# Bar rows built at a quarter of their width and earlier on GpSimd, with a thinner fill of the value tile

## The chip, the cores and the metric

One core of a Trainium2 chip runs the whole program. The metric is the device time of one execution in microseconds; the number compared is the median over several executions. A profile is one further execution, seen instruction by instruction.

## The reference

The input x is 8 sequences of 512 tokens with 128 channels. It is normalised, and two branches read the result:

```
xn = layernorm(x)                                # 8 x 512 x 128
s  = attention(xn): Q,K,V = relu(xn @ W + b); 16 heads of 8 channels,
     causal softmax, times V, plus xn, normalised again, gamma, beta
g  = silu(ffn(xn)): second norm, @ attn_w.T + b + residual,
     8 experts (128 -> 512 -> 128, gelu), @ next_w.T + b, gelu
out = x + s * g
```

The top-k of the router in the reference is computed and not used. Keys and queries whose row of xn sums to exactly zero are masked.

## The kernel before

The program has two stages with a barrier between them. In stage one (to about 183 us of the span) the statistics and normalised rows of x are made, then for each of the 8 sequences (i = 0 to 7) the projections Q, K and V, the split of Q and K into three bf16 parts that are stored to DRAM, and the whole feed-forward branch. In stage two the attention runs, 32 units of four heads. Each engine has its instruction order written out by hand, and semaphores join the engines. GpSimd and VectorE also wait on themselves after nearly every instruction (`link`).

**Causal mask.** Instead of a mask on the scores, 48 extra rows ("bar rows") are appended to the contraction of queries and keys. `bar_k` and `bar_q` hold them, 48 x 512 bf16 each. The pattern depends only on the token's place within its tile of 128, so the four tiles (TB = 4) are alike. `bar_rows` fills each with a constant and then overwrites it by `below`, an `affine_select`, three times for `bar_k` and four times for `bar_q`. Their only reader is `load_fixed` on SyncE, which waits for `bars_ready` when i is 1.

**GpSimd in stage one**, in order: constants, two identity matrices, a fill of `v_all` with 1.0 (L298) and then the release of `consts`, for which TensorE (two) and ScalarE (one) wait; seven linked operations on the bias rows (L312 to L318); `second_roots` for the first group of 8 tiles (twelve small operations that start once VectorE has sent `seeds_ready`); `bar_rows`; then `totals(i)`, six small operations that end in `sums_ready`. `v_all` is 128 x 32 x 144 in float32: for each head 8 value columns and one column of ones. ScalarE writes the value columns later (L574).

**VectorE in stage one**, in order: mean, variance and roots of the first 8 tiles, `quotients(0)`, `second_seeds`, `sums(0)`, `quotients(1)`, `sums(1)`, `rests` of sequence 0 (L484), means of the other 24 tiles (L91 to L401), `lows` of sequence 0 (L491, waits for ScalarE's L603), then variances and roots of the 24 tiles (from L408), and from there sequence by sequence.

**ScalarE and TensorE.** After the first projections ScalarE copies V out (L574) and waits for `sums_ready` before `second_norm(0)` (L536). TensorE then transposes that (L630), and multiplies (L649, L652); ScalarE adds the bias (L554), and the experts follow (L697, L707 on TensorE, L597 and L603 on ScalarE). At i = 1 TensorE runs 28 and 40 products without use (`hold`, L662), which keep it busy while it waits for VectorE.

Of the kernel before, what the change touches and what calls it, by code (L numbers as in the profile page):

```python
# [17 lines left out]
ALU = mybir.AluOpType  # L18
# [3 lines left out]
P = 128  # L22
B, T, C = 8, 512, 128
HEADS, DH = 16, 8
# [3 lines left out]
TB = T // P  # L28
# [8 lines left out]
VW = DH + 1  # L37
# [3 lines left out]
BLOCK = 3  # L41
BAR_ROWS = 48
# [3 lines left out]
BAR_KEYS = (0.0, 2.0 ** -37, 2.0 ** 13, 2.0 ** 63)  # L46
BAR_QUERIES = (-2.0 ** 62, -2.0 ** 12, -2.0 ** -38)
# [57 lines left out]
def build_program(nc, ctx, x, wq, wk, wv, wattn, wnext, w1, w2, cols, rows, out):  # L105
    def sb(name, shape, dt=F32, where=ctx):
        return where.enter_context(nc.sbuf_tensor(name, shape, dt))

    def sem(name):
        return ctx.enter_context(nc.semaphore(name))  # L110
# [12 lines left out]
    v_all = sb("v_all", [P, NT, HEADS * VW])  # L123
# [5 lines left out]
    bar_q = sb("bar_q", [BAR_ROWS, T], BF16)  # L129
    bar_k = sb("bar_k", [BAR_ROWS, T], BF16)  # L130
# [34 lines left out]
    def load_mask(sp, b, par, g, done):  # L165

        src = mask_dram[bass.ds(b * TB, TB), :].rearrange("n t -> (n t)")
        sp.dma_start(kx[par][MROW:MROW + 1, g],
                     src.unsqueeze(0).unsqueeze(0).broadcast_to([1, G, T])).then_inc(done, 16)
# [13 lines left out]
    with ExitStack() as one:  # L183
# [40 lines left out]
        blank, consts = sem("blank"), sem("consts")  # L224
# [20 lines left out]
        mean, var, a, y, t, s, sh, sl, r, nr, rem, v2, y2, t2 = (small[:, k, :] for k in range(14))  # L245

        with nc.Block() as block:
# [37 lines left out]
            @block.gpsimd  # L285
            def _(pool):
                pool.memset(ident[:, :], 0.0).then_inc(blank, 1)
                pool.memset(ident_b[:, :], 0.0).then_inc(blank, 1)
                pool.memset(ones_p[:, :], 1.0).then_inc(blank, 1)
                pool.memset(ones_b[:, :], 1.0).then_inc(blank, 1)  # L290
                pool.memset(bias_rows[:, :, :], 0.0).then_inc(blank, 1)
                pool.memset(q_fixed[:, :, :], 0.0).then_inc(blank, 1)
                pool.wait_ge(blank, 6)
                pool.memset(q_fixed[:, 0, :], 1.0).then_inc(blank, 1)
                for t in (ident, ident_b):
                    pool.affine_select(out=t[:, :], in_=t[:, :], compare_op=ALU.not_equal, fill=1.0, base=0,
                                       pattern=[[-1, P]], channel_multiplier=1).then_inc(blank, 1)
                pool.memset(v_all[:, :, :], 1.0).then_inc(blank, 1)  # L298
                pool.wait_ge(blank, 10)
                pool.sem_inc(consts, 2)  # L300

                chain = [0]

                def link(ins):
                    chain[0] += 1
                    ins.then_inc(pool_self, 1)
                    pool.wait_ge(pool_self, chain[0])


                pool.wait_ge(rows_in, 16)  # L310
                both = rows_sb[:, 0:2, :]
                link(pool.tensor_copy(bias_part[:, 0], both))  # L312
                link(pool.tensor_tensor(bias_rest[:, :, :], both, bias_part[:, 0], ALU.subtract))
                link(pool.tensor_copy(bias_part[:, 1], bias_rest[:, :, :]))
                link(pool.tensor_tensor(bias_part[:, 2], bias_rest[:, :, :], bias_part[:, 1], ALU.subtract))
                for p in range(PARTS):
                    on_p = slice(32 * p, 32 * p + 1)
                    link(pool.tensor_copy(bias_rows[on_p, :, :], bias_part[on_p, p]))  # L318
                pool.sem_inc(bias_ready, 1)

                def below(bar, k, value, sign=1):

                    link(pool.affine_select(out=bar[:, :].rearrange("p (n t) -> p n t", t=P),
                                            in_=bar[:, :].rearrange("p (n t) -> p n t", t=P),
                                            compare_op=ALU.is_ge, fill=value, base=-k * sign,
                                            pattern=[[0, TB], [sign, P]], channel_multiplier=-BLOCK * sign))

                def bar_rows():

                    link(pool.memset(bar_k[:, :], BAR_KEYS[BLOCK]))  # L330
                    for k in range(BLOCK, 0, -1):
                        below(bar_k, k, BAR_KEYS[k - 1])
                    link(pool.memset(bar_q[:, :], BAR_QUERIES[BLOCK - 1]))
                    for k in range(BLOCK - 1, -1, -1):
                        below(bar_q, k, BAR_QUERIES[k - 1] if k > 0 else 0.0)
                    below(bar_q, BLOCK - 1, 0.0, -1)
                    pool.sem_inc(bars_ready, 1)

                tt = pool.tensor_tensor

                def second_roots(tok, group):

                    at = slice(group[0], group[0] + group[1])
                    pool.wait_ge(seeds_ready, tok.next(seeds_ready))
                    for _ in range(3):
                        link(tt(t2[:, at], y2[:, at], y2[:, at], ALU.mult))
                        link(tt(t2[:, at], t2[:, at], v2[:, at], ALU.mult))
                        link(pool.tensor_scalar(t2[:, at], t2[:, at], -0.5, 1.5, ALU.mult, ALU.add))
                        link(tt(y2[:, at], y2[:, at], t2[:, at], ALU.mult))

                def totals(tok, i):

                    at = slice(TB * i, TB * i + TB)
                    pool.wait_ge(lanes_ready, tok.next(lanes_ready))
                    v = s16[:, at, :].rearrange("p n (a b l) -> p n a b l", a=2, b=2)
                    link(tt(s8[:, at, :, :], v[:, :, :, 0, :], v[:, :, :, 1, :], ALU.add))  # L356
                    link(tt(s4[:, at, :], s8[:, at, 0, :], s8[:, at, 1, :], ALU.add))
                    v = s4[:, at, :].rearrange("p n (a b) -> p n a b", b=2)
                    link(tt(s2[:, at, :], v[:, :, :, 0], v[:, :, :, 1], ALU.add))
                    link(tt(rem[:, at], s2[:, at, 0], s2[:, at, 1], ALU.add))  # L360
                    link(pool.tensor_scalar(shift[:, at], rem[:, at], -1.0 / C, None, ALU.mult))
                    link(tt(shift[:, at], shift[:, at], y2[:, at], ALU.mult))
                    pool.sem_inc(sums_ready, 1)

                tok = Tokens(pool)
                for i in range(B):
                    if i == 0:
                        second_roots(tok, GROUPS[0])
                        bar_rows()
                    if i == 2:  # L370
                        second_roots(tok, GROUPS[1])
                    totals(tok, i)
                pool.wait_ge(maskT_ready, 1)
                pool.dma_start(mask_dram, maskT[:, :]).then_inc(mask_out, 16)
                pool.wait_ge(mask_out, 16)
                for g in range(NG):
                    load_mask(pool, 0, 0, g, mask_in)
                pool.wait_ge(mask_in, 16 * NG)
                for g in range(NG):
                    pool.sem_inc(stack_in[0][g], 16)  # L380

                pool.sem_inc(blank, -10)
# [879 lines left out]
```

## Time and profile before

| | us |
|---|---|
| median of 3 executions | 456.26 (455.87 to 466.83) |
| the profiled execution's own time | 457.67 |
| its span, first to last instruction | 455.6 |
| TensorE busy | 383.3 (84%) |
| VectorE busy | 373.1 (82%) |
| ScalarE busy | 289.2 (63%) |
| GpSimd busy | 179.1 (39%) |
| mean granted TensorE clock | 0.970 |

The span starts at 0 with the first instruction; all times of rows count from there. Busy shares are averages over both stages. PE is TensorE, ACT ScalarE, DVE VectorE, POOL GpSimd.

### The profile page before, as it was taken

How to read it: one execution, taken by the hardware profiler on the slowest of the kernel's cores; microseconds unless marked ns; L12 is line 12 of the kernel's file. 1: busy time of each engine (PE TensorE's matmuls, PEld its weight loads, DVE VectorE, ACT ScalarE, POOL GpSimd, SP SyncE). 2: the span in 40 equal slices, each digit the busy share in tenths (PEclk: the TensorE clock that was granted, in tenths of full speed). 3: DMA queues.
4: the chain of work that ended last, by engine and by line, in shares of the span. 5: the costliest groups of instructions: out<-in, count | busy, mean ns of one | idle time of the engine just before them, and what ended most of it. 6: DMA issues, size and time to landing. Idle time of an engine off the chain costs nothing.

```text
span 455.6 us, 9692 instructions
## 1 busy us (share of the span) xinstructions
PE 383.3 (84%) x3541; PEld 249.3 (55%) x3541; DVE 373.1 (82%) x865; ACT 289.2 (63%) x580; POOL 179.1 (39%) x446
## 2 busy tenths in 40 slices
PE   0041899889999998899999999999999999999850
PEld 0021575457877775456656656665666566566420
DVE  5899388977778921899899999898999998989427
ACT  0122481278898884167777877877778778778740
POOL 9237000411111002311236547456556383565591
PEclk9997599999999999999999999999999999999995
DMA  8910030077644534723233342423332424340000
GB/s 238 316 52 1 0 100 0 0 170 160 156 112 115 139 98 116 128 57 86 81 90 79 82 109 73 118 63 105 92 96 64 129 56 113 79 110 27 4 24 23
DMA packets 31413, 41.72 MB, mean 92 GB/s; under 512 B 5910, under 2 KB 23686, under 8 KB 31366
## 3 DMA queue, kind: packets, MB, share of 16 engines
q1 hardware_dynamic: 31206, 41.08, 34.6%
q8 instruction: 28, 0.46, 0.4%
q14 instruction: 19, 0.16, 0.1%
q0 software_dynamic: 160, 0.03, 0.0%
HBM read 26.43 MB, written 11.02 MB: 82 GB/s over the span
## 4 chain that ended last, share of the span: by engine, by line
PE 43%; DVE 13%; issue 2%; ACT 1%; POOL 1%; DVEq 0%; ACTq 0%; POOLq 0%
PE banks L1152 15%; PE banks L1135 8%; DVE mx L951 8%; PE banks L1115 8%; PE banks L1117 5%; PE banks L1137 5%; DVE stats L996 2%; PE banks L1162 2%; DVE res L990 1%; ACT pt L1070 1%; PE banks L1124 0%; DVE res L977 0%; DVE res L980 0%; DVE mixed L981 0%; DVE aggr L1000 0%
## 5 line engine op out<-in xcount | busy, mean ns | idle before, releaser
L951 DVE TENSOR_REDUCE mx<-banks 128x1 f32<-128x512 f32 (+3 forms) x352 | 200.0, 633 | 19.9 <-PE banks L1117 18.2
L1070 ACT ACTIVATE pt<-banks 128x512 f32<-128x512 f32 x320 | 169.2, 601 | 44.2 <-PE banks L1137 36.7
L1152 PE MATMUL banks<-pt,vg 128*18 128x512 f32 (+3 forms) x1024 | 81.4, 436 | 0.7 <-ACT pt L1070 0.7
L1115 PE MATMUL banks<-k_own,q_own 76*128 76x384 bf16 (+2 forms) x192 | 48.4, 274 | 5.4 <-DVE mx L951 2.7
L1115 PE MATMUL banks<-w_room 76*128 76x384 bf16 (+2 forms) x192 | 48.1, 274 | 3.3 <-DVE mx L951 3.3
L842 POOL TENSOR_SCALAR mneg<-mx 128x16 f32<-128x16 f32 x32 | 8.1, 254 | 107.7 <-DVE mx L951 106.6
L1135 PE MATMUL banks<-w_room 76*128 76x384 bf16 (+2 forms) x192 | 47.5, 275 | 0.9 <-ACT pt L1070 0.5
L1135 PE MATMUL banks<-q_own,k_own 76*128 76x384 bf16 (+2 forms) x192 | 47.8, 274 | 0.0
L1152 PEld LDWEIGHTS banks<-pt,vg 128*18 128x18 f32 x1024 | 23.7, 97 | 43.8 <-issue 33.4
L1117 PE MATMUL banks<-k_own,q_own 124*128 124x128 bf16 x256 | 44.0, 219 | 0.0
L1117 PE MATMUL banks<-w_room 124*128 124x128 bf16 x256 | 43.8, 219 | 0.0
L1137 PE MATMUL banks<-q_own,k_own 124*128 124x128 bf16 x256 | 42.5, 219 | 0.0
L1137 PE MATMUL banks<-w_room 124*128 124x128 bf16 x256 | 42.2, 219 | 0.0
L697 PE MATMUL banks<-xaT,w_room 128*128 128x256 f32 x128 | 31.3, 401 | 0.8 <-ACT xaT L554 0.8
L707 PE MATMUL banks<-hid,w_room 128*128 128x256 f32 x128 | 29.2, 380 | 2.7 <-ACT hid L597 2.7
L624 PE MATMUL banks<-ident,xn_all 128*128 128x128 f32 x32 | 5.3, 292 | 27.9 <-DVEq L455 27.9
L697 PEld LDWEIGHTS banks<-xaT,w_room 128*128 128x128 f32 x128 | 25.2, 202 | 5.9 <-ACT xaT L554 2.4
L491 DVE TENSOR_TENSOR parts<-rest,parts 128x512 bf16<-128x512 f32 x16 | 11.1, 693 | 20.4 <-ACT parts L603 19.9
L707 PEld LDWEIGHTS banks<-hid,w_room 128*128 128x128 f32 x128 | 24.2, 190 | 6.4 <-ACT hid L597 3.2
L1115 PEld LDWEIGHTS banks<-k_own,q_own 76*128 76x128 bf16 x192 | 18.4, 97 | 16.5 <-DVE mx L951 8.9
L597 ACT ACTIVATE hid<-banks,cols_sb 128x256 f32<-128x256 f32 x64 | 26.1, 476 | 2.1 <-PE banks L697 1.9
L356 POOL TENSOR_TENSOR s<-s 128x32 f32<-128x32 f32 x8 | 2.4, 301 | 63.5 <-DVE s L470 63.1
(175 smaller groups left out, 764.3 us busy)
## 6 DMA issues: line engine op xcount, KB each, us to landing
k_scratch<-parts SPq DMA_DIRECT2D x40, 128.0 KB, 2.4
k_own<-k_scratch SPq DMA_DIRECT2D x48, 96.0 KB
w_room<-k_scratch SPq DMA_DIRECT2D x48, 96.0 KB
q_scratch<-parts SPq DMA_DIRECT2D x24, 128.0 KB, 2.4
q_own<-q_scratch SPq DMA_DIRECT2D x32, 96.0 KB
w_room<-q_scratch SPq DMA_DIRECT2D x32, 96.0 KB
w_room<-in_w_dram SPq DMA_DIRECT2D x1, 2048.0 KB, 9.1
q_own<-q_scratch SPq DMA_DIRECT2D x16, 112.0 KB
```

What stands on the lines that cost most here:

```text
L491: link(tt(parts[:, i % 2, o, 2, :], rest[:, o, :], parts[:, i % 2, o, 1, :], ALU.subtract))
L597: ins = act.activation(hid[:, h, j, :], banks[:, bank + j // 2, EC * (j % 2):EC * (j % 2) + EC], ACT.Gelu, bias=b1[2 * n + h][j])
L697: ins = mm(banks[:, bank + j // 2, EC * (j % 2):EC * (j % 2) + EC], w1_sb[:, 2 * n + h, P * j:P * j + P], xaT[:, EC * h:EC * h + EC], star ...
L707: ins = mm(banks[:, XB, EC * h:EC * h + EC], w2_sb[:, 2 * n + h, j, :], hid[:, h, j, :], start=(j == 0), stop=(j == HC - 1))
L951: dve.tensor_reduce(mx[:, u % 2, heads[0]:heads[-1] + 1, q], banks[:, S0 + slots[0] % SLOTS, 0:w * len(heads)].rearrange("p (h k) -> p h k ...
L996: ins = dve.bn_stats(stats[:, k, :], res[:, k, :])
L1070: act.activation(pt[:, T * j:T * j + T], banks[:, bank(), :], ACT.Exp, scale=SCALE).then_inc(exp_done, 1)
L1115: mm(o[:, 0:w - P], qx[by][0:LIVE, g, h, P * q:P * q + P], kx[by][0:LIVE, g, h, 0:w - P], start=True, stop=True)
L1117: ins = mm(o[:, w - P:w], qx[by][0:STACK, g, h, P * q:P * q + P], kx[by][0:STACK, g, h, w - P:w], start=True, stop=True)
L1135: mm(o[:, P:n], kx[par][0:LIVE, g, h, P * k:P * k + P], qx[par][0:LIVE, g, h, P * k + P:T], start=True, stop=True)
L1137: ins = mm(o[:, 0:P], kx[par][0:STACK, g, h, P * k:P * k + P], qx[par][0:STACK, g, h, P * k:P * k + P], start=True, stop=True)
L1152: ins = mm(banks[32 * h:32 * h + VP, OT, P * k:T], vg[:, g, k, h, :], pt[:, KPLACE[k, h]:KPLACE[k, h] + n], start=(k == 0 and g % 2 == 0), ...
```

## The change

The affine selects and fills of the bar rows work on the first 128 of 512 columns only. For each of the two tiles one copy on GpSimd then repeats these columns over the other 384; both copies run before a single wait. The call of `bar_rows` moves from behind `second_roots` of the first group to a place right behind the bias rows, ahead of every wait for VectorE. The fill of `v_all` writes only the column of ones of each head, 32 x 16 = 512 elements per partition with a distance of 9 elements, instead of all 4608.

```
-                pool.memset(v_all[:, :, :], 1.0).then_inc(blank, 1)
+                pool.memset(v_all[:, :, :].rearrange("p n (h w) -> p n h w", w=VW)[:, :, :, DH], 1.0).then_inc(blank, 1)
...
                 def below(bar, k, value, sign=1):
 
-                    link(pool.affine_select(out=bar[:, :].rearrange("p (n t) -> p n t", t=P),
-                                            in_=bar[:, :].rearrange("p (n t) -> p n t", t=P),
-                                            compare_op=ALU.is_ge, fill=value, base=-k * sign,
-                                            pattern=[[0, TB], [sign, P]], channel_multiplier=-BLOCK * sign))
+                    link(pool.affine_select(out=bar[:, 0:P], in_=bar[:, 0:P], compare_op=ALU.is_ge, fill=value,
+                                            base=-k * sign, pattern=[[sign, P]], channel_multiplier=-BLOCK * sign))
 
                 def bar_rows():
 
-                    link(pool.memset(bar_k[:, :], BAR_KEYS[BLOCK]))
+                    link(pool.memset(bar_k[:, 0:P], BAR_KEYS[BLOCK]))
                     for k in range(BLOCK, 0, -1):
                         below(bar_k, k, BAR_KEYS[k - 1])
-                    link(pool.memset(bar_q[:, :], BAR_QUERIES[BLOCK - 1]))
+                    link(pool.memset(bar_q[:, 0:P], BAR_QUERIES[BLOCK - 1]))
                     for k in range(BLOCK - 1, -1, -1):
                         below(bar_q, k, BAR_QUERIES[k - 1] if k > 0 else 0.0)
                     below(bar_q, BLOCK - 1, 0.0, -1)
+                    for bar in (bar_k, bar_q):
+                        ins = pool.tensor_copy(bar[:, P:T].rearrange("p (n t) -> p n t", t=P),
+                                               bar[:, 0:P].unsqueeze(1).broadcast_to([BAR_ROWS, TB - 1, P]))
+                    link(ins)
                     pool.sem_inc(bars_ready, 1)
 
+                bar_rows()
                 tt = pool.tensor_tensor
...
                     if i == 0:
                         second_roots(tok, GROUPS[0])
-                        bar_rows()
```

## Rows read from the trace of the kernel before

**Rows 1.** Timeline of GpSimd: start us, duration us, instruction, idle before it and its releaser.
```profile
4.62 0.28 POOL L296 TENSOR_SCALAR_AFFINE_SELECT ident_b<-ident_b 128x128 bf16<-128x128 bf16 x1
4.86 3.93 POOL L298 MEMSET v_all<- 128x4608 f32 x1
...
29.18 0.20 POOL L346 TENSOR_TENSOR small<-small 128x8 f32<-128x8 f32 x1 [14.56 <-DVEq L465]
...
33.67 0.52 POOL L330 MEMSET bar_k<- 48x512 bf16 x1
...
37.29 2.92 POOL L323 TENSOR_SCALAR_AFFINE_SELECT bar_q<-bar_q 48x512 bf16<-48x512 bf16 x4
40.40 0.34 POOL L356 TENSOR_TENSOR s<-s 128x32 f32<-128x32 f32 x1 [0.18 <-POOL bar_q L323]
```

**Rows 2.** Timeline of ScalarE, sequence 0, then its counterparts in sequences 1 and 2.
```profile
35.63 0.60 ACT L574 ACTIVATE v_all<-banks 128x512 f32<-128x512 f32 x1 [0.87 <-PE banks L643]
43.35 1.65 ACT L536 ACTIVATE xl_st<-xn_all,shift,small 128x128 f32<-128x128 f32 x4 [7.12 <-POOLq L363]
...
50.85 0.69 ACT L554 ACTIVATE xaT<-banks,cols_sb 128x512 f32<-128x512 f32 x1 [3.87 <-PE banks L652]
...
58.23 0.63 ACT L603 ACTIVATE parts<-rest 128x512 bf16<-128x512 f32 x1
...
64.88 0.69 ACT L554 ACTIVATE xaT<-banks,cols_sb 128x512 f32<-128x512 f32 x1 [1.12 <-PE banks L652]
...
105.49 0.66 ACT L603 ACTIVATE parts<-rest 128x512 bf16<-128x512 f32 x1
```

**Rows 3.** Timeline of TensorE, sequence 0, then later sequences and the products of `hold`.
```profile
27.91 1.08 PE L624 MATMUL banks<-ident,xn_all 128*128 128x128 f32 x4 [27.91 <-DVEq L455]
...
33.68 1.91 PE L643 MATMUL banks<-wv_sb,xnT 128*128 128x128 f32 x8
45.05 1.12 PE L630 MATMUL banks<-ident,xl_st 128*128 128x128 f32 x4 [9.46 <-ACT xl_st L536]
47.04 2.07 PE L649 MATMUL banks<-xlT,wattn_sb 128*128 128x512 f32 x2 [0.87 <-ACT xlT L548]
...
51.59 5.86 PE L697 MATMUL banks<-xaT,w_room 128*128 128x256 f32 x16 [0.78 <-ACT xaT L554]
...
62.96 1.02 PE L649 MATMUL banks<-xlT,wattn_sb 128*128 128x512 f32 x2
...
81.58 1.99 PE L707 MATMUL banks<-hid,w_room 128*128 128x256 f32 x8 [2.69 <-ACT hid L597]
83.41 8.80 PE L662 MATMUL banks<-bias_rows,ones_p 128*128 128x512 bf16 x40
94.30 0.65 PE L630 MATMUL banks<-ident,xl_st 128*128 128x128 f32 x4 [2.10 <-ACT xl_st L536]
...
100.88 3.62 PE L697 MATMUL banks<-xaT,w_room 128*128 128x256 f32 x16
```

**Rows 4.** Timeline of VectorE up to the variances of the second group.
```profile
7.33 1.49 DVE L401 TENSOR_SCALAR small<-small 128x8 f32<-128x8 f32 x1
...
33.20 1.14 DVE L452 SCALAR_TENSOR_TENSOR gate_all<-qlo,small,gate_all 128x128 f32<-128x128 f32 x4
...
38.36 2.26 DVE L452 SCALAR_TENSOR_TENSOR xn_all<-gate_all,small,quo 128x128 f32<-128x128 f32 x4
...
49.84 0.18 DVE L401 TENSOR_SCALAR small<-small 128x24 f32<-128x24 f32 x1
...
59.72 3.36 DVE L408 TENSOR_TENSOR xn_all<-x_all,small 128x3072 f32<-128x3072 f32 x1
```

**Rows 5.** Windows A:B: length, busy PE, PEld, DVE, ACT, POOL (x), granted clock, DMA share, GB/s.
```profile
36.00:38.90 2.90, 0.00 (x0) 0.00 (x0) 2.83 (x8) 0.23 (x1) 2.48 (x5) 1.00 0.00 0
39.00:55.90 16.90, 9.20 (x18) 5.38 (x19) 10.41 (x12) 5.72 (x11) 4.91 (x14) 0.50 0.00 0
56.00:181.00 125.00, 119.17 (x573) 85.36 (x571) 90.67 (x221) 87.89 (x186) 18.52 (x53) 1.00 0.42 105
```

## The prediction, made before the changed kernel was run

> **What bounds the kernel now.** The busy shares of the page say nothing about this change: TensorE and VectorE are above 80% over the whole span, but the touched work lies in the first 60 us. So I read the timeline of each engine there. GpSimd first [rows 1]: it idles 14.56 us before the small roots, then runs them, then the bar rows from 33.67 to about 40.2, and only then the first totals (40.40 to about 43.3). ScalarE next [rows 2]: it has finished V at 36.23 and stands idle 7.12 us until 43.35, released by GpSimd. TensorE [rows 3]: last product of V at 35.59, next instruction at 45.05, idle 9.46 us, waiting for ScalarE. VectorE has slack at this point, because it has the means of the second group to do until 50.02, but then it too waits, for ScalarE's L603, and begins the second group's variances at 59.72 [rows 4]. So between 36 and 60 us the path is GpSimd's bar rows, totals, ScalarE, TensorE, ScalarE, VectorE. The bar rows stand on it with their full length, although nobody needs their result until after 90 us.
>
> Behind 59.72 everything hangs on VectorE or, later, on TensorE, which is busy 119.17 of the 125 us from 56 to 181 [rows 5]. The two `hold` blocks have fixed lengths and sit between events that both shift with this chain, and stage two starts at a barrier behind it. What 59.72 gains, the end gains, unless the order of arrivals changes.
>
> **The bar rows leave the path.** They occupy 40.40 - 33.67 = 6.73 us of GpSimd, waits between instructions included [rows 1]. Taken out, the totals run 33.67 to 36.62 at their old length (43.35 - 40.40 = 2.95), and ScalarE starts L536 at 36.62. What is late next is ScalarE itself, free at 36.23, only 0.4 us sooner; so even faster totals would add no more than that. Gain at this point 6.73.
>
> **Their new place.** The idle stretch begins at 29.18 - 14.56 = 14.62 in the kernel before. The fill of `v_all` shrinks from 4608 to 512 elements: 3.93 us times 512/4608 is 0.44; a filled row of 512 took 0.52 [rows 1], which I take. That a strided fill costs more per element no row shows; if it cost as much as the whole old fill, nothing would be lost against before, and TensorE doesn't start before 27.91 [rows 3]. With it the bias rows start about 3 us earlier. A select over 128 columns took 0.28 [rows 1], one over 512 costs 2.92/4 = 0.73 with its wait; so seven small ones with 0.08 of wait cost 2.5, two fills 0.6, two copies of 384 between 0.8 and 1.6 (less and more than a 512-wide select each). The bar rows then take 4 to 5 us somewhere between 9 and 17 us. 12 us of room stay before 29.18, so even at the old 6.73 GpSimd waits for nothing it didn't wait for before.
>
> **What hides them has a price.** VectorE runs its first statistics there and stands alone on the path: TensorE waits for it until 27.91 [rows 3]. Rows show that the two engines disturb each other. VectorE's L401 on 128x8 took 1.49 us and ended at 8.82, right behind the fill of `v_all` (8.79); the same on 128x24 took 0.18 [rows 1, 4]. The shorter fill gives this back: 1.3 us, on the path. Against it: the bias operations move forward onto VectorE's small sums; they collided with other work of it in before as well, and I charge 0.5 more. And the selects: while the wide ones ran, three series of VectorE's L452 went from 34.34, where the one before them ended, to 38.36 + 2.26 = 40.62: 6.3 us where three series of 1.14 with their gaps take 3.5, so 2.7 us lost with the rounding over about 6 us of bar rows [rows 1, 4]. At the same rate the 4.5 us of narrow bar rows cost 2.0; at none, if short ones fit between, 0. Part of them falls on a reduction, whose collisions no row here settles. I take 1.1. Sum for the first statistics: -1.3 + 0.5 + 1.1 = +0.3 us, ends -0.8 and +1.2.
>
> The Trainium skill (page "SBUF — State Buffer", section on engine ports) has a rule that speaks against this move: VectorE and GpSimd share a port pair as an exclusive lock, and whoever comes second blocks fully for the whole instruction. The L401 row agrees; the L452 rows agree in kind only, since they lost less than the time that the selects ran.
>
> **The clock.** This is the largest open term. TensorE ran at its lower level (1.2 GHz) through the first products: the column says 1.00 there, but eight products of 128 columns took 1.91 us [rows 3], and I go by durations. The column reads 1.00 from 36.0 to 38.9, 0.50 from 39.0 to 55.9 and 1.00 after that [rows 5]: the upper level had been granted by the end of the burst that ended at 35.59, was never used, and was lost again about 3.3 us into the 9.46 us of idleness. All of sequence 0's work from 45.05 to 56 ran at 1.2 GHz. With the change TensorE's next instruction comes at 45.05 - 6.73 = 38.3, after 2.7 us of idleness. At 81.58 the engine had been idle 2.69 us and the clock stayed up [rows 3, 5]. So the likeliest case is that the upper level survives and the rest of sequence 0 runs on it. Its worth from rows of either level: L630 1.12 against 0.65, 0.5; L649 to the end of L652 47.04 to 50.85 against 62.96 to 64.88, 1.9; first L697 to the end of the second L603 51.59 to 58.86 against 100.88 to 106.15, 2.0, less 0.2 because sequence 0 also has a table load there [rows 2, 3]. Sum 4.2. Then the second L603 ends 43.35 to 58.86 = 15.51, less 4.2 = 11.3 after L536, at 36.62 + 11.3 = 47.9.
>
> **What is late next.** VectorE reached the end of the means at 50.02; without the 2.7 us of collisions at 47.3, say 47.5 with the roots and totals of GpSimd still beside it. Its two L491 (0.69 each) then run 47.5 to 49.0, and the variances start at 49.1 instead of 59.72: 10.6. If the lower level holds, the second L603 ends at 36.62 + 15.51 = 52.1, the variances start at 53.0, and the gain is 6.7.
>
> **Sum.** Upper level: -10.6 + 0.3 = -10.3. Against the profiled execution 457.67 - 10.3 = 447.4 (span 445.3). That execution is 1.4 above the median of the runs shown, which I use as the base: 456.26 - 10.3 = 446.0.
>
> **Rivals.**
> 1. *The clock drops in the shorter gap or never rose.* The rise came just at the end of the burst [rows 3, 5], so in another execution it may not come, and 2.7 us is at the edge of what a row shows to be survived. Then the gain is 6.7 - 0.3 = 6.4: 449.9. For it: the rise had no margin. Against: the surviving gap at 81.58.
> 2. *The lock at full price.* If every narrow operation holds VectorE up for its whole length, the bar rows cost the sum of their durations without waits: seven selects of 0.28, two fills of about 0.2 and two copies of at least 0.3 make 3.0. The first statistics then lose -1.3 + 0.5 + 3.0 = 2.2 instead of 0.3, and the end is at 447.9 at the upper level of the clock and 451.8 at the lower. Against: 2.7 us lost beside seven wide selects of 0.73 with their waits. The port rule named above, on the Trainium skill's page "SBUF — State Buffer", is this rival.
> 3. *The bar rows weren't the wait.* If the totals of sequence 0 were late for VectorE's sums instead, nothing would come. The release row (40.40 behind `bar_q`) speaks against it [rows 1]; 456, small.
> 4. *The other side: the second `hold` at the lower level.* TensorE idles 2.69 us before 81.58, then runs L707 and 40 products in 1.99 + 8.80 us [rows 3]. If TensorE now gains more than VectorE, this gap grows; once it reaches about 3.3 us, where the clock fell at 38.9, these take 21.6 instead of 10.8 us and end at 103 instead of 92.2, 8.7 after 94.30, when L630 was due. With a first part at the lower level (-6.4) the sum is +2.3: 458.6. It decides when the gap grows by 0.6 us. Against: both ends of the gap shift by 10 to 11 us, within 0.4 of each other.
>
> **How the numbers follow.** Upper level 0.47; lower level 0.34; lock at full price 0.10; no effect 0.04; hold at the lower level 0.05. A difference of about 2% (9.1 us, 447.1) is what a measurement of this kernel tells from no change. The upper level gives more than that if the first statistics lose less than 1.5 us, nearly always: faster 0.46, within 2% 0.52, slower 0.02 (458.6 is itself within 2%). The likeliest case alone spans 444.8 (-0.8, and 0.4 of quicker totals) to 447.2; with the lower level, +1.2 and its rounding, up to 450.8. The range 444.3 to 451.3 leaves out the last two rivals and the worst of the second.
>
> **What would show it.** GpSimd: a fill near 0.5, nine short bar operations and two copies done before 17 us, the first total right behind L349. ScalarE: L536 near 36.9, idle before it under 1 us. TensorE: L630 near 38.6 after some 2.7 us of idleness; four of them in 0.65 and L649 plus L652 in 1.9 if the upper level held, 1.12 and 3.8 if not. VectorE: L401 at 0.2; first products of TensorE at 28.2, within 27.1 and 29.1; L408 of the second group near 49.4 or 53.3. Wrong would be: bar rows that reach beyond 29, TensorE's first product past 29.5, a gap before the second `hold` beyond 3 us with a granted clock of 0.50 behind it, or a shift at 59.72 that is not there at 183.

## The result and the profile after

The changed kernel took 449.7 us (median of four; three of them from 448.24 to 449.74, the fourth 459.58), the profiled one 449.74 with a span of 447.7. The ratio to the kernel before is 0.985, 95% interval 0.9805 to 0.9895: 1.5% faster, where 446.0, 2.2% faster, was forecast. In part of the executions of either kernel the TensorE clock drops once more at the barrier between the stages, which costs some 8 us, and ratios leave these executions out except where the text says otherwise.

GpSimd after the change (timeline, columns as in [rows 1]):

```profile
4.86 1.01 POOL L298 MEMSET v_all<- 128x512 f32 x1
...
8.52 3.27 POOL L318 COPY bias_rows<-bias_part 1x256 bf16<-1x256 bf16 x3
11.94 0.20 POOL L328 MEMSET bar_k<- 48x128 bf16 x1 [0.16 <-POOL bias_rows L318]
12.29 1.09 POOL L323 TENSOR_SCALAR_AFFINE_SELECT bar_k<-bar_k 48x128 bf16<-48x128 bf16 x3
13.45 0.20 POOL L331 MEMSET bar_q<- 48x128 bf16 x1
13.79 1.44 POOL L323 TENSOR_SCALAR_AFFINE_SELECT bar_q<-bar_q 48x128 bf16<-48x128 bf16 x4
15.29 0.53 POOL L336 COPY bar_k<-bar_k 48x384 bf16<-48x384 bf16 x1
15.78 0.50 POOL L336 COPY bar_q<-bar_q 48x384 bf16<-48x384 bf16 x1
29.01 0.20 POOL L349 TENSOR_TENSOR small<-small 128x8 f32<-128x8 f32 x1 [12.74 <-DVEq L467]
...
33.52 0.25 POOL L359 TENSOR_TENSOR s<-s 128x32 f32<-128x32 f32 x1
```

The bar rows now run from 11.94 to 16.28 and the first total follows the small roots at once, at 33.52 instead of 40.40. ScalarE after the change (against [rows 2]):

```profile
35.13 0.60 ACT L576 ACTIVATE v_all<-banks 128x512 f32<-128x512 f32 x1 [0.54 <-PE banks L645]
35.63 1.64 ACT L538 ACTIVATE xl_st<-xn_all,shift,small 128x128 f32<-128x128 f32 x4
...
42.66 0.69 ACT L556 ACTIVATE xaT<-banks,cols_sb 128x512 f32<-128x512 f32 x1 [3.87 <-PE banks L654]
...
50.27 0.63 ACT L605 ACTIVATE parts<-rest 128x512 bf16<-128x512 f32 x1
```

TensorE after the change (against [rows 3]):

```profile
27.74 1.08 PE L626 MATMUL banks<-ident,xn_all 128*128 128x128 f32 x4 [27.74 <-DVEq L457]
...
33.51 1.59 PE L645 MATMUL banks<-wv_sb,xnT 128*128 128x128 f32 x8
37.31 0.66 PE L632 MATMUL banks<-ident,xl_st 128*128 128x128 f32 x4 [2.22 <-ACT xl_st L538]
38.84 2.08 PE L651 MATMUL banks<-xlT,wattn_sb 128*128 128x512 f32 x2 [0.87 <-ACT xlT L550]
...
43.40 6.11 PE L699 MATMUL banks<-xaT,w_room 128*128 128x256 f32 x16 [0.78 <-ACT xaT L556]
...
73.62 1.99 PE L709 MATMUL banks<-hid,w_room 128*128 128x256 f32 x8 [2.68 <-ACT hid L599]
75.45 8.80 PE L664 MATMUL banks<-bias_rows,ones_p 128*128 128x512 bf16 x40
```

VectorE after the change (against [rows 4]):

```profile
7.96 0.53 DVE L403 TENSOR_SCALAR small<-small 128x8 f32<-128x8 f32 x1
8.52 1.22 DVE L410 TENSOR_TENSOR xn_all<-x_all,small 128x1024 f32<-128x1024 f32 x1
...
46.95 0.18 DVE L403 TENSOR_SCALAR small<-small 128x24 f32<-128x24 f32 x1
...
51.77 3.36 DVE L410 TENSOR_TENSOR xn_all<-x_all,small 128x3072 f32<-128x3072 f32 x1
```

And three windows of it (columns as in [rows 5]):

```profile
34.00:38.00 4.00, 1.75 (x11) 1.33 (x10) 3.75 (x14) 2.72 (x7) 1.12 (x5) 1.00 0.01 2
38.00:42.00 4.00, 3.16 (x4) 1.18 (x4) 3.71 (x4) 0.78 (x1) 2.18 (x6) 0.50 0.00 0
...
46.00:50.00 4.00, 4.00 (x15) 3.26 (x15) 1.68 (x6) 3.00 (x8) 0.00 (x0) 0.72 0.00 0
```

Read together: the wait for GpSimd is gone (L538 starts as soon as ScalarE is free, 7.72 us sooner), TensorE idles only 2.22 us before L632, and L632 still runs at 2.4 GHz (0.66, as at 94.30 in [rows 3]). But then the granted clock is 0.50, and L651 takes 2.08 for two products, as at 47.04 in [rows 3]. So the upper level outlived the 2.22 us, was used for one group of transposes, and was lost within the 0.87 us of waiting behind them, at 38.0. It comes back only within the window 46 to 50.

The same points of the program in both kernels, and where the forecast had them:

| us | before | after | shift | forecast shift |
|---|---|---|---|---|
| TensorE's first transposes | 27.91 | 27.74 | -0.17 | +0.3 |
| second norm, L536 / L538 | 43.35 | 35.63 | -7.72 | -6.4 |
| end of the second L603 / L605 | 58.86 | 50.90 | -7.96 | -10.7 |
| variances of the second group | 59.72 | 51.77 | -7.95 | -10.3 |
| first maxima of stage two, L951 / L953 | 183.98 | 176.06 | -7.92 | -10.3 |
| end of the span | 455.6 | 447.7 | -7.9 | -10.3 |

Everything is decided between 27 and 52 us; the shift at 51.77 arrives whole at the end, and stage two lasts 271.6 us in both. The start of the second norm gained more than forecast, the stretch behind it almost nothing.

### The profile page after: what moved, and what is told of

Same layout as the page of the kernel before. It is cut to its first block, busy times and chain, and to the rows that moved or that the text cites. A ratio compares the mean times of both kernels' runs of the same rounds, so it can differ in the third digit from the quotient of the medians.

```text
span 447.7 us, 9695 instructions
## 1 busy us (share of the span) xinstructions
PE 382.7 (85%) x3541; PEld 249.0 (56%) x3541; DVE 370.2 (83%) x865; ACT 289.1 (65%) x580; POOL 173.5 (39%) x448
## 4 chain that ended last, share of the span: by engine, by line
PE 44%; DVE 13%; issue 2%; ACT 1%; POOL 1%; DVEq 0%; ACTq 0%; POOLq 0%
PE banks L1154 15%; PE banks L1137 8%; DVE mx L953 8%; PE banks L1117 8%; PE banks L1119 5%; PE banks L1139 5%; DVE stats L998 2%; PE banks L1164 2%; DVE res L992 1%; ACT pt L1072 1%; PE banks L1126 0%; DVE res L979 0%; DVE res L982 0%; DVE mixed L983 0%; DVE aggr L1002 0%
## 5 line engine op out<-in xcount | busy, mean ns | idle before, releaser
L953 DVE TENSOR_REDUCE mx<-banks 128x1 f32<-128x512 f32 (+3 forms) x352 | 200.1, 636 | 19.9 <-PE banks L1119 18.2
L1137 PEld LDWEIGHTS banks<-w_room 76*128 76x128 bf16 x192 | 18.7, 97 | 14.8 <-ACT pt L1072 6.3
```

The source lines that it names most:

```text
L953: dve.tensor_reduce(mx[:, u % 2, heads[0]:heads[-1] + 1, q], banks[:, S0 + slots[0] % SLOTS, 0:w * len(heads)].rearrange("p (h k) -> p h k ...
L1137: mm(o[:, P:n], kx[par][0:LIVE, g, h, P * k:P * k + P], qx[par][0:LIVE, g, h, P * k + P:T], start=True, stop=True)
```

## The experiments

### The parts of the change

**The fill alone.**

```
-                pool.memset(v_all[:, :, :], 1.0).then_inc(blank, 1)
+                pool.memset(v_all[:, :, :].rearrange("p n (h w) -> p n h w", w=VW)[:, :, :, DH], 1.0).then_inc(blank, 1)
```

> The kernel before with the thin fill of v_all alone. Path theory (the gain is the time taken off GpSimd's work between 36 and 60 us of the path, the fill gives back only what VectorE waited for it): TensorE's first product at 27.1 to 27.3 instead of 27.91, ScalarE's L536 at 42.6, time lower by 0.6 to 0.8 us, ratio 0.998. Rival (the fill is what paid in the whole change, through VectorE's collisions): lower by 2 us or more.

Ratio 0.998 (0.995 to 1.001); TensorE's first transposes at 27.28, L536 at 42.72, both 0.63 sooner. As the path theory had it: the fill gives VectorE back what it waited for, and no more.

**The wide bar rows moved early.** The call alone moves; fill and width stay.

```
                     for i in range(B):
                         if i == 0:
                             second_roots(tok, GROUPS[0])
-                            bar_rows()
...
+                bar_rows()
                 tt = pool.tensor_tensor
```

> The kernel before with bar_rows moved ahead of the first statistics at its old width of 512 columns, full fill. Path theory with collisions: L536 no longer waits for the bar rows (6.7 us gained), but seven wide selects beside VectorE's roots and quotients cost up to 2.7 us, TensorE's first product at 28.5 to 30.6, time lower by 4 to 6 us, ratio 0.987 to 0.991. Rival (collisions cost nothing beside small instructions): first product at 27.9, lower by 6.7 to 7.1. Rival (the narrow width is what paid): no gain.

The first transposes came at 30.80, 2.89 us late, L536 at 38.58, the second group's variances at 54.72, stage two's first maxima at 178.94: 5.0 us sooner than before, within the 4 to 6. All seven executions (459.2 to 461.0) had the drop at the barrier, going by their mean granted clock (0.945 to 0.957, the profiled one among them, against 0.97), so the ratio 1.008 (1.005 to 1.011), which sets them against executions of the kernel before without it, says nothing; the kernel before with it took 462.5 to 466.9. The verdict rests on the rows. VectorE's roots beside GpSimd's wide selects, two timelines of this kernel, GpSimd first:

```profile
15.45 2.13 POOL L323 TENSOR_SCALAR_AFFINE_SELECT bar_k<-bar_k 48x512 bf16<-48x512 bf16 x3
```

```profile
15.36 0.17 DVE L85 TENSOR_TENSOR small<-small 128x8 f32<-128x8 f32 x1
15.56 0.54 DVE L82 TENSOR_TENSOR small<-small 128x8 f32<-128x8 f32 x1
16.14 0.17 DVE L83 TENSOR_TENSOR small<-small 128x8 f32<-128x8 f32 x1
16.34 0.54 DVE L84 TENSOR_SCALAR small<-small 128x8 f32<-128x8 f32 x1
```

Every second small operation takes 0.5 instead of 0.17: one gets through, the next is held up for about the rest of a select. Moving the wide rows early costs 2.9 us of the 6.7 that it takes off the path, so it pays.

**The narrow bar rows at their old place.** Width and copies of the change, old call, old fill.

```
-                bar_rows()
                 tt = pool.tensor_tensor
...
                         second_roots(tok, GROUPS[0])
+                        bar_rows()
```

(against the changed kernel, with the full fill of `v_all` put back)

> The kernel before with the bar rows at 128 columns and two copies, at their old place behind the first roots, full fill. Path theory: the bar rows last 4.3 us instead of 6.7, L536 comes 2.4 us sooner, time lower by 2.2 to 2.6 us, ratio 0.995. Rival (the move is all, since the wait is on something else at that place): no change.

L538 came at 41.43, 1.92 us sooner where 2.4 was expected; that row, and not the time, speaks against the rival. The ratio 0.996 (0.990 to 1.002) doesn't exclude no change. It takes in two executions with the drop at the barrier (460.3 and 460.4); the six without it took 453.8 to 456.0, against 455.7 to 458.3 of the kernel before. The variances of the second group came at 55.63, 4.1 us sooner: 2.2 us more than L538 gained, because in this profiled execution the clock was back at 48.3 instead of 55.9.

**The wide bar rows moved later**, behind the totals of sequence 1, full fill.

```
                     if i == 0:
                         second_roots(tok, GROUPS[0])
+                    if i == 2:
                         bar_rows()
-                    if i == 2:
                         second_roots(tok, GROUPS[1])
```

> The kernel before with the wide bar rows moved the other way, behind the totals of sequence 1, full fill. Path theory: they are off the path there too, and nothing collides with the first statistics; TensorE's first product stays at 27.91, L536 at 36.2 (bounded by ScalarE's copy of V), variances of the second group 7.1 us sooner, time lower by 6.8 to 7.3 us, ratio 0.985, as good as the whole change. Rival (the early place, or the thin fill, carries the gain): lower by 4 us or less.

Ratio 0.9825 (0.980 to 0.985), L536 at 36.12, the first transposes unchanged at 27.91. The variances came at 50.22, 9.5 us sooner and not 7.1: in this profiled execution the clock was down for 3.4 us only, from 39.1 to 42.5, and the expectation counted on no gain from the clock. An unchanged `bar_rows` moved off the path is as good as the whole change. Neither the quarter width, nor the copies, nor the fill is needed for the gain.

### The clock behind the short wait

All kernels from here on carry 20 instead of 10 products at the end of stage one, which takes the drop at the barrier out of most executions and makes the rest comparable with each other. They are not free, as the next run shows.

```
-IDLE_PRODUCTS = 10
+IDLE_PRODUCTS = 20
```

On the kernel before:

> The kernel before with 20 instead of 10 products without use at the end of stage one, so that TensorE idles about 0.4 us instead of 2.56 at the barrier. Theory that the executions at 462 to 467 us are those in which the clock drops behind that idle stretch and stays at 1.2 GHz for some 24 us: all executions at 455.6 to 458.3, none at 462 or above. Rival (the slow executions have another cause, in DMAs or elsewhere): as before, more than half at 462 to 467.

On the changed kernel:

> The changed kernel with the same 20 products. If the barrier is the only place where executions part: all at 448.0 to 450.3, 7.5 to 8.0 us under the kernel before with 20 products. Rival (the change moved stage one against the drop, so part of its gain or loss sits there): a difference from the kernel before with 20 products outside 6.5 to 8.5 us.

Of 12 executions of the kernel before with 20 products 10 took 455.9 to 458.9 and 2 took 465.5 and 467.5; of 25 of the kernel before itself, run beside it, 16 lay above 463. So the drop became rare, not absent: the theory holds in kind, and what causes the remaining two is open. The ten are a little slower than the kernel before, ratio 1.003 (1.001 to 1.006). In the profiled one, and in three more of the seven profiles with 20 products, SyncE's last five stores took 4.16 to 4.44 us instead of 3.10, for which the barrier waits; none of the six profiles with 10 products has that. Whether the added products bring it about is not shown.

The changed kernel with 20 products had 4 of 6 at 447.7 to 450.7, ratio 0.985 (0.981 to 0.989), the other two above 457, so the expectation that all would lie below 450.3 missed. Between the undisturbed ones of both kernels with 20 products there are 8.0 us (medians 456.9 and 448.9), so the change's gain doesn't sit at the barrier.

The profiled execution of the kernel before with 20 products also shows that the first drop isn't of one length there: 13.6 us instead of 17.0, variances of the second group at 57.73 instead of 59.72.

What the drop at the barrier looks like is seen in the wide-moved-early kernel, windows of it with the columns of [rows 5], stage two starting at 178.53:

```profile
180.00:184.00 4.00, 4.00 (x20) 2.32 (x18) 3.56 (x7) 0.00 (x0) 0.77 (x4) 0.50 0.93 155
184.00:194.00 10.00, 10.00 (x48) 5.79 (x47) 7.76 (x12) 1.55 (x2) 1.09 (x5) 0.50 0.21 36
194.00:204.00 10.00, 10.00 (x66) 6.86 (x67) 7.58 (x13) 5.54 (x10) 1.09 (x5) 0.51 0.16 47
204.00:208.00 4.00, 4.00 (x51) 2.07 (x46) 2.48 (x5) 2.56 (x5) 1.08 (x5) 1.00 0.16 42
```

TensorE is busy without a gap for some 24 us and the clock stays at 0.50 all the while.

**Products in the short wait of the changed kernel.**

```
                 projections(tok, 0)
+                hold(8)
                 second_normed(tok, 0)
```

> The changed kernel with 20 products, and 8 more right behind the first product of V, in the 2.2 us for which TensorE waits for the second norm of sequence 0. Theory that my prediction failed because the clock dropped behind this short idle stretch: the granted clock stays up, L651 and L654 take 0.51 per product, the second L605 ends at 46.9, VectorE's lows are bound by its own means (47.1), the second group's variances start at 48.7 instead of 51.8, and the time is 3.1 us under the changed kernel with 20 products, ratio near 0.975 to before. Rival (the clock is not lost through idleness but could not be held there): no change, or up to 1 us slower by the added products.

TensorE, ScalarE and VectorE of this kernel, three timelines, then one window of it and SyncE's last five stores:

```profile
34.78 1.89 PE L664 MATMUL banks<-bias_rows,ones_p 128*128 128x512 bf16 x8
37.44 0.66 PE L632 MATMUL banks<-ident,xl_st 128*128 128x128 f32 x4 [0.77 <-ACT xl_st L538]
38.97 1.12 PE L651 MATMUL banks<-xlT,wattn_sb 128*128 128x512 f32 x2 [0.87 <-ACT xlT L550]
39.93 1.02 PE L654 MATMUL banks<-xnT,ident 128*128 128x512 f32 x2
41.73 3.72 PE L700 MATMUL banks<-xaT,w_room 128*128 128x256 f32 x16 [0.78 <-ACT xaT L556]
```

```profile
46.44 0.66 ACT L605 ACTIVATE parts<-rest 128x512 bf16<-128x512 f32 x1
```

```profile
47.23 0.18 DVE L403 TENSOR_SCALAR small<-small 128x24 f32<-128x24 f32 x1
47.44 1.53 DVE L493 TENSOR_TENSOR parts<-rest,parts 128x512 bf16<-128x512 f32 x2
49.12 3.36 DVE L410 TENSOR_TENSOR xn_all<-x_all,small 128x3072 f32<-128x3072 f32 x1
```

```profile
34.00:42.00 8.00, 5.58 (x25) 2.83 (x25) 7.45 (x18) 4.83 (x10) 3.45 (x11) 1.00 0.00 1
```

```profile
165.56 4.33 SPq L269 DMA_DIRECT2D k_scratch<-parts  x5
```

This is the course that the prediction described for the changed kernel: from L538 (35.74) to the end of the second L605 (47.10) 11.36 us, VectorE no longer waiting but bound by its own means, variances at 49.12, 10.60 sooner than before. The time fell less than the row promises: 447.2 to 449.9, ratio 0.983 (0.981 to 0.986), about 1 us instead of 3 under the changed kernel with 20 products (medians 448.0 and 448.9, ranges that overlap). Two things take the rest. The changed kernel's own cost of the drop varies between executions: with 20 products its profiled one had the variances at 49.57 already, after a drop of under 4 us, where the profiled one shown above had 51.77. And in this kernel's profiled execution SyncE's last five stores took 4.33 us, against 3.12 in the changed kernel and 3.10 before: of the 10.60 us at the variances 9.28 are left at stage two's first maxima (174.70).

**Three products instead of eight.**

```
                 projections(tok, 0)
+                hold(3)
                 second_normed(tok, 0)
```

> The changed kernel with 20 products at the barrier and 3 instead of 8 in TensorE's short wait, which leaves about 1.5 us idle instead of 0.8. If any product there is enough: as with 8, variances at 49.1, 447.2 to 449.9. If the idle time must be short: in between, some executions with a granted clock of 0.50 from about 38, 448 to 450.

447.75 to 449.04, ratio 0.979 (0.973 to 0.986). The profiled one idled 1.35 us before L632, and L651 still took 2.08: the clock had dropped once more, for under 4 us, and the variances came at 49.97, between 49.12 and 51.77. The times don't tell three products from eight: the medians are 447.9 and 448.0.

**Products in the long wait of the kernel before**, without any of the change.

```
                 projections(tok, 0)
+                hold(34)
                 second_normed(tok, 0)
```

> The kernel before with 20 products, and 34 more in its 9.46 us wait for the second norm; nothing of the change. Clock theory: sequence 0 runs at 2.4 GHz behind the bar rows, 4.2 us less from L536 to the second L603, time 4.2 us under the kernel before with 20 products. Rival (the products run long past 45 because the clock isn't up when they start): a gain of less than 2 us, or a loss.

12 of 12 at 452.8 to 456.9, median 454.5 against 456.9 of the undisturbed ones with 20 products alone: 2.5 us, not 4.2. Against the kernel before itself the ratio is 0.997 (0.994 to 1.000), 1.3 us. In its profiled execution the products ended at 42.80, the clock dropped after them, and L649 took 2.08 again; from L536 to the end of the second L603 it took 12.85 us, against 15.51 before [rows 2], 13.49 with 20 products alone and 11.36 with the clock held, and the variances came at 56.28, against 59.72 and 57.73. So the clock's part is there in the kernel before too, it is the smaller one, and its size depends on which execution it is set against.

### Together

**Narrow bar rows later, clock held.** The changed kernel with 20 products, `hold(8)` in the short wait, and the call of `bar_rows` behind the totals of sequence 1.

```
-                bar_rows()
                 tt = pool.tensor_tensor
...
                     if i == 2:
+                        bar_rows()
                         second_roots(tok, GROUPS[1])
```

> The changed kernel with 20 products at the barrier, 8 in TensorE's short wait, and the narrow bar rows moved to behind the totals of sequence 1 instead of ahead of the first statistics. Theory that the narrow bar rows still cost VectorE 0.7 us in its first roots: TensorE's first product at 27.1 to 27.3 instead of 27.74 to 27.95, the second group's variances 0.6 to 0.8 us sooner than with the bar rows early (48.4 against 49.1), time lower by as much. Rival (short operations fit between VectorE's and cost nothing): no difference in TensorE's first product.

The first transposes came at 27.13 and the variances at 48.30. At the later place the bar rows (41.10 to 45.41) ran beside VectorE's long reduction L91, which took 5.37 us, as in the kernel with eight products, where nothing of them ran beside it (5.37; 5.29 in the changed kernel). The four kernels with the narrow bar rows early have 27.74, 27.77, 27.87 and 27.95, so the narrow rows cost VectorE 0.6 to 0.8 us where the change puts them. 447.2 to 448.9, ratio 0.978 (0.971 to 0.986); the median is 0.6 below that of the kernel with eight products, which is within the spread of either.

**With the first projections warmed up too.**

```
                 tok = Tokens(pe)
+                pe.wait_ge(bias_ready, 1)
+                hold(46)
                 normed(tok, 0)
...
                 projections(tok, 0)
-                hold(8)
+                hold(22)
```

> As the kernel with narrow bar rows behind the totals of sequence 1, but with 46 products ahead of TensorE's first transposes and 22 in its wait for the second norm, so that the first projections run at 2.4 GHz too. Clock theory: the four projections take 4 us instead of 7.8, ScalarE is done with V at about 32, but L538 stays where GpSimd's totals put it (34.7 to 35.4) and VectorE's means still bind the variances at about 48.4: no gain in the fastest execution, but less spread, all at 446 to 448. Rival (the earlier projections move the path): lower by 1 us or more.

446.3 to 447.4, median 446.6, ratio 0.976 (0.970 to 0.983): the fastest of all, with the least spread. As expected the path hardly moves (L538 at 34.83, variances at 48.22); the median is 0.8 us lower. The warming itself worked in part only, in the profiled execution. TensorE, timeline:

```profile
12.69 12.52 PE L664 MATMUL banks<-bias_rows,ones_p 128*128 128x512 bf16 x46 [12.69 <-DMA cols_sb<-in_cols_dram]
26.95 0.66 PE L626 MATMUL banks<-ident,xn_all 128*128 128x128 f32 x4 [1.74 <-DVEq L457]
28.29 2.07 PE L638 MATMUL banks<-xnT,wq_sb 128*128 128x512 f32 x2 [0.69 <-ACT xnT L546]
```

The 46 products brought the upper level, the first transposes ran on it (0.66), but behind 1.74 and 0.69 us of waiting the granted clock was 0.50 from 27.9 to 31.3, and the first of the projections still took 2.07. Only the later ones ran faster, and ScalarE was done with V at 33.5, not 32.

## Why the prediction was right or wrong

**The bar rows leave the path: right.** Forecast 6.73 for the start of the second norm, and at most 0.4 more. Measured 7.72, of which 0.17 came from the statistics. The totals ran 33.52 to 35.44, 1.9 us instead of 2.95. Before, their last two took 0.78 and 0.73 us beside VectorE's L484 (41.69 to 43.21); now they took 0.23 and 0.39 and L486 ran later, from 38.80. That L484 held them up is read from this coincidence. ScalarE was done with V half a microsecond sooner, by the 0.17 and since the clock rose while L645 ran (1.59 against 1.91), so the bound of 0.4 was too tight. The kernel with the wide rows moved later shows that this term is the change.

**The price at their new place: right in kind, too high by 0.5.** Forecast -1.3 + 0.5 + 1.1. The fill alone gave -0.63 for the first two terms (-0.8 forecast); the strided fill took 1.01, not 0.52, and L403 still 0.53. The narrow rows cost 0.5 to 0.8 (against 27.28 and 27.13), not 1.1: together -0.17 instead of +0.3. The rival of the lock at full price (3.0 for the narrow rows) is refuted by that number, and 2.9 us for the wide rows early, with 5.0 us of selects, say the same. The Trainium skill (page "SBUF — State Buffer", section "Who interferes with whom") has the second of the two engines blocked until the first is done, and names the kinds of VectorE operation that this concerns, which the prediction left out. The traces agree for the single instruction that is caught; beside the wide selects only about every second one was.

**The clock: the step that failed.** "So the likeliest case is that the upper level survives" rested on one gap of 2.69 us that the clock had borne later. It was lost behind 2.22 us and one group of transposes, and in another kernel behind 1.35 and the same. Nor was the surviving gap a safe witness for itself. The same gap, behind the same 28 products, stands in every kernel; here it is in the kernel before and in the changed kernel, each with 20 products at the barrier, one line of each timeline and a window of the second:

```profile
79.60 1.99 PE L707 MATMUL banks<-hid,w_room 128*128 128x256 f32 x8 [2.95 <-ACT hid L597]
```

```profile
71.45 2.52 PE L709 MATMUL banks<-hid,w_room 128*128 128x256 f32 x8 [2.96 <-ACT hid L599]
```

```profile
72.80:76.00 3.20, 3.20 (x9) 1.34 (x9) 3.09 (x12) 0.00 (x0) 0.96 (x5) 0.50 0.00 0
```

The first kept the clock and the second lost it. Over all profiles the clock was kept behind 2.68, 2.69 and twice 2.95 us there, and lost behind 2.93 to 2.96 us five times and behind longer gaps four times. So neither the length of one idle stretch nor the dense products ahead of it decides the outcome alone; what does is open.

The kernel with eight products shows both that this was the failing step and what it was worth: with the clock held (1.00 from 34 to 42) the variances shift by 10.60. The forecast had 10.3, and 10.6 without the term of the statistics, which was +0.04 there. The changed kernel's profiled execution got 7.95 of it, so the term was 2.65 in that execution and 0.45 in the luckiest that was profiled. The time of the kernel with eight products, 448.0, is still 2.0 above the forecast 446.0: the late stores are part of that in its profiled execution (448.5), and the next point is another part.

**The base of the sum: too low for its rows.** The rows come from an execution of 457.67 with the clock down for 17.0 us, and the gain read from them was taken off the median 456.26. The kernel before has executions at 455.7 to 456.5 and at 457.7 to 458.3; the profile with 20 products, with 13.6 us of low clock and its variances 2.0 us sooner, fits the lower ones once its late stores (1.3 us) are taken off. In such an execution part of the clock's term is already there and can't be gained again. That all the lower ones are of this kind is an inference from one profile.

**The size of the clock's term.** Its ceiling, 4.2 from L536 to the second L603, is right (15.51 before, 11.36 held). But the forecast treated it as all or nothing. The drop lasted 10.2 us in the profiled execution of the changed kernel, 17.0 before, and 3.4 in four other kernels, so intermediate results were the common ones. The lower-level case of the first rival (449.9) is nearly what was measured (449.7), but by luck: it had a shift of 6.4, and the profiled execution has 7.95, since the second norm began 1.3 us sooner than the rival assumed; the two times meet only because the rival's is counted from 456.26 and not from 457.67. The ends given for the likeliest case are also a little off: 456.26 - 10.6 - 0.8 - 0.4 is 444.5, not 444.8, and 456.26 - 10.6 + 1.2 is 446.9, not 447.2.

**Stage two and the two `hold` blocks: right for the changed kernel.** The gap before the second block stayed at 2.68 with the clock up. But the last rival's condition was no rare one: in nine of the 13 profiles the clock did drop there. Its price was too high: in the kernel with eight products the gap was 4.12 us, L710 took 3.23 instead of 1.99 and the 40 products 9.29 instead of 8.80, since the clock was back after 3.4 us, and TensorE still waited for its next input afterwards (0.40 us instead of 2.09).

## What to carry to other kernels

Look for who waits behind a piece of work, before making it cheaper: here an unchanged `bar_rows` moved to an idle stretch did all that the narrowed one did, and the better stretch was the one in which VectorE ran one long reduction, which took 5.37 us with the bar rows beside it and without. When a wait on the path is shortened, write down what state the clock will be in behind it; if TensorE comes up only just before a wait, a few products without use inside the wait are a cheap test. One surviving gap in a trace is one draw, not a threshold: look for the same gap in the profiles of other kernels. And take a gain off the time of the execution whose rows it was read from.

## What was not expected of the hardware

- The upper clock level was lost behind 2.22 and 1.35 us of idleness with a group of transposes behind them, and, after 46 dense products, behind 1.74 and 0.69 us. Behind the same 28 dense products it was kept after 2.69 and twice 2.95 us and lost after 2.93 to 2.96 us five times.
- After the drop at the barrier TensorE worked without a gap for 24 us and stayed at 0.50 (20 to 24 us in the four profiles with this drop). The products there contract over 76 or 124 rows in bf16, mostly 128 to 512 columns long. In stage one the clock came back after 17 us at the latest, with fp32 products and pauses between them.
- A fill of 512 fp32 elements with a distance of 9 elements took 1.01 us: 2.0 ns per element, against 0.85 ns in the contiguous fill of 4608 (3.93 us) [rows 1].
- Three GpSimd copies of 256 bf16 elements in one partition (L318), 1.41 us before, took 3.27 us beside VectorE's two long subtractions and products (L410, L411): GpSimd loses time beside VectorE too.
